# Two attentions as straight-line code, with row maxima planned closer to their use

## What is computed

```python
x = x + _layernorm(_L0_attn_ref(_layernorm(x), w_q, w_k, w_v, w_o))
x = x + _layernorm(_L0_ffn_ref(_layernorm(x), gate_w, gate_s, up_w, up_s, down_w, down_s))
x = x + _layernorm(_L1_attn_ref(_layernorm(x), Wqkv, Wo))
x = x + _layernorm(_L1_ffn_ref(_layernorm(x), W, b, A, B, p_scores))
```

## Time and profile before

| | us |
|---|---|
| median of 3 runs | 2366.73 (2365.27 to 2372.2) |
| the profiled execution, its own time | 2357.78 |
| its span, first to last instruction | 2356.0 |
| B, from the first row product (184) to 938 | 754 |
| G, from the first row product (1536) to 2145 | 609 |
| D, feed-forward of layer 0 | 460 |
| VectorE / ScalarE / TensorE busy | 1475 / 1146 / 2092 |

### The profile page before, as it was taken

The page is one execution under the profiler, slowest core; times in us unless marked ns, Lnnn a source line. Parts: engine busy times, 40 slices in busy tenths (PEclk is TensorE's granted clock), DMA queues, the critical chain, the costliest instruction groups (busy, mean ns, idle before and its releaser), DMA issues. The chain is left out here.

```text
span 2356.0 us, 39663 instructions
## 1 busy us (share of the span) xinstructions
PE 2091.7 (89%) x13072; PEld 1233.5 (52%) x13072; DVE 1475.3 (63%) x2004; ACT 1146.4 (49%) x2399; POOL 134.0 (6%) x171
## 2 busy tenths in 40 slices
PE   7987999999999998869999995789898989998785
PEld 5763333333333332748888874545455555545564
DVE  5317988887888882754333315367676666753677
ACT  3211777776777777223222211226665656663153
POOL 0000000000000000210000000000000000000203
PEclk9995999999999999979999997969998889986888
DMA  5443422422332310342100003421111111101411
GB/s 205 161 148 42 61 36 34 58 38 33 51 46 33 47 23 13 113 152 68 37 1 36 4 16 129 146 53 35 37 47 32 39 44 27 47 3 54 144 66 72
DMA packets 100890, 143.37 MB, mean 61 GB/s; under 512 B 32084, under 2 KB 43220, under 8 KB 100720
## 3 DMA queue, kind: packets, MB, share of 16 engines
q1 hardware_dynamic: 99520, 138.91, 23.2%
q10 hardware_dynamic: 832, 1.41, 0.4%
q0 software_dynamic: 384, 0.77, 0.1%
HBM read 93.45 MB, written 47.05 MB: 60 GB/s over the span
## 5 line engine op out<-in xcount | busy, mean ns | idle before, releaser
L730 DVE TENSOR_REDUCE maxesB<-s_psB 128x1 f32<-128x1024 f32 x512 | 603.1, 1220 | 116.3 <-PE s_psB L779 115.4
L714 ACT ACTIVATE probsB<-st_psB 128x512 f32<-128x512 f32 x1024 | 528.9, 603 | 171.5 <-PE st_psB L793 171.3
L730 DVE TENSOR_REDUCE maxesG<-s_psG 128x1 f32<-128x896 f32 (+7 forms) x512 | 368.9, 754 | 185.0 <-PE s_psG L764 180.5
L714 ACT ACTIVATE probsG<-st_psG 128x512 f32<-128x512 f32 (+3 forms) x768 | 335.0, 492 | 244.0 <-PE st_psG L764 180.4
L793 PE MATMUL st_psB<-q_stackB,k_stackB 50*128 50x512 f32 x1024 | 401.0, 474 | 17.2 <-ACT probsB L714 6.8
L779 PE MATMUL s_psB<-k_stackB,q_stackB 48*128 48x512 f32 x1024 | 336.7, 449 | 31.7 <-DMA k_stackB<-k_parts 18.7
L779 PE MATMUL s_psG<-k_stackG,q_stackG 52*128 52x512 f32 (+3 forms) x768 | 263.9, 426 | 65.3 <-DVE maxesG L730 38.8
L793 PE MATMUL st_psG<-q_stackG,k_stackG 54*128 54x512 f32 (+3 forms) x768 | 315.1, 463 | 6.2 <-ACT probsG L714 4.5
L779 PEld LDWEIGHTS s_psB<-k_stackB,q_stackB 48*128 48x128 f32 x1024 | 162.7, 196 | 283.8 <-DVE maxesB L730 235.9
L815 PE MATMUL o_psB<-probsB,v_onesB 128*32 128x512 f32 x2048 | 279.0, 613 | 0.0
L793 PEld LDWEIGHTS st_psB<-q_stackB,k_stackB 50*128 50x128 f32 x1024 | 169.6, 187 | 135.7 <-ACT probsB L714 132.4
(11 more groups left out here) (241 smaller groups left out, 2925.1 us busy)
## 6 DMA issues: line engine op xcount, KB each, us to landing
q_stackB<-q_parts SPq DMA_DIRECT2D x186, 64.0 KB
k_stackB<-k_parts SPq DMA_DIRECT2D x93, 128.0 KB
q_stackG<-q_parts SPq DMA_DIRECT2D x186, 64.0 KB
q_parts<-partsA SPq DMA_DIRECT2D x16, 512.0 KB, 2.8
k_parts<-partsA SPq DMA_DIRECT2D x16, 512.0 KB, 2.8
q_parts<-partsF SPq DMA_DIRECT2D x16, 512.0 KB, 2.8
k_stackG<-k_parts SPq DMA_DIRECT2D x93, 64.0 KB
xA<-in_x SPq DMA_DIRECT2D x4, 1024.0 KB
```

The costliest lines, as they stand in the source:

```text
L714: act.activation(probs[:, (i % ring) * GH + h, first:HALF], st_ps[:, bank_of(n), first:HALF], ACT.Exp).then_inc(st_used, 1)
L730: dve.reduce_max(maxes[:, half, h * QT + qt:h * QT + qt + 1], s_ps[:, n % 2, 0:key_width(half, qt)], AX.X).then_inc(maxed, 1)
```

## The change

- `run`, `body` and all loops of `attention` are gone: all 16 groups are written out, and every wait is on a constant.
- One list of steps and one of row units goes over all groups. `plan_units` gives each unit a weight (its width + 140), spreads them evenly over all steps, and starts so early that a half's maxima are ready `LEAD` = 3 steps ahead. This places 22 units ahead of the first step in B and 30 in G, then two a step in B; in G the steps of a group have 2, 6, 4, 3, 3, 2, 3, 2, 2, 1, 2, 2 units. The first unit of group `it+1` (number 32 * (it+1), for it of 1 and more) falls in step 5 of group `it` in B and in step 1 of group `it` in G. `turn_max` comes in steps 5 and 13 in B, and in G in step 1 (for half 1 of the same group) and step 5 (for half 0 of the next). For the first half of all it comes after all units that are ahead of the first step.
- `s_ps` is four slots of 512; a unit up to 512 wide takes one.
- `step_order` issues row, key and mask products by which side of the array is free; a key's masks may stand apart from it. In B the order of a step becomes R0, K2, R0', K3, K0, R1, K1, R1' (R row, K key product); before it was R0, K2, R0', K3, R1, K0, R1', K1.
- In G the row masks of TensorE go. VectorE adds a constant `ramp` (128 x 1024 float32, zero but for the mask in its last 128 columns) and takes the maximum in one operation, `tensor_tensor_reduce`, whose element output goes to `junk` in bf16. `ramp` is a new constant of 512 KB, loaded at the program's start behind `ident`.
- The copies of `o_ps` go to ScalarE in G. `v_ones` has two buffers.
- SyncE loads the stacks of group `it+1` in group `it` (before: `it+2`), once the last key product of group `it-1` is made, then V, and only then writes the rows of half 1. Group 0 loads none beside the first two.

```diff
+LEAD = 3
+FIXED = 140
+LOWEST = -3.0e38
+JUNK = 8
...
+    s_ps = ps(f"s_ps{tag}", [P, 4, HALF], F32)
+    st_ps = ps(f"st_ps{tag}", [P, n_st, HALF], F32)
...
+    def plan_units():
+
+
+        work = [key_width(t % 2, qt) + FIXED for t, qt, _ in units]
+        done = list(itertools.accumulate(work))
+        group = first_of[2]
+        per_step = done[2 * UNITS - 1] / group
+        ahead = max(done[UNITS * (t + 1) - 1] - per_step * max(first_of[t] - LEAD, 0) for t in range(1, 3))
+        ahead = max(ahead, done[UNITS - 1])
+        at = [[] for _ in steps]
+        before = []
+        for n, d in enumerate(done):
+            i = int(-(-(d - ahead) // per_step)) - 1
+            (before if i < 0 else at[min(i, len(steps) - 1)]).append(n)
+        return before, at
+
+    before, units_at = plan_units()
...
+    def step_order(i):
+
+
+        _, _, _, first, diagonal = steps[i]
+        chunks = [(n, k) for n in units_at[i] for k in range(len(row_parts(*units[n][:2])))]
+        keys = [[], []]
+        for h in range(GH):
+            keys[h // GS] += [("key", h)] + [("mask", h, a) for a in range(2) if diagonal]
+        n_rows, n_keys = max(len(chunks), 1), len(keys[0]) + len(keys[1])
+        out, free = [], [0, 0]
+        while chunks or any(keys):
+            row_side = units[chunks[0][0]][2] // GS if chunks else None
+            u = 0 if free[0] <= free[1] else 1
+            if row_side != u and not keys[u]:
+                u = 1 - u
+            rows_left, keys_left = len(chunks) / n_rows, (len(keys[0]) + len(keys[1])) / n_keys
+            if row_side == u and (rows_left >= keys_left or not keys[u]):
+                n, k = chunks.pop(0)
+                out.append(("row", n, k))
+                a, b = row_parts(*units[n][:2])[k]
+                cost = b - a
+            else:
+                out.append(keys[u].pop(0))
+                cost = HALF - first if out[-1][0] == "key" else SIDE * (out[-1][2] + 1)
+            free[u] = max(free[u], min(free)) + cost
+        return out
+
...
+    turn_after = {}
+    for t in range(TURNS):
+        i = max([j for j, ns in enumerate(units_at) if any(units[n][0] == t for n in ns)], default=-1)
+        if i >= 0:
+            turn_after[i + 1] = turn_after.get(i + 1, []) + [t]
+    early_turns = [t for t in range(TURNS) if not any(t in ts for ts in turn_after.values())]
...
-            def body(it, buf, before):
-                if before:
-                    sp.wait_ge(st_made, 1 + n_takes * it)
-                max_rows(2 * it + 1, 1, buf)
-                if not is_last(it, 2):
-                    sp.wait_ge(stacks, n_loads * (it + 2))
-                    settle(sp, sp_passed)
-                    load_stacks(sp, it + 2, (buf + 2) % 3)
-                if not is_last(it):
-                    sp.wait_ge(v_set, it + 2)
-                    settle(sp, sp_passed)
-                    load_v(it + 1)
-                if not is_last(it):
-                    max_rows(2 * it + 2, 0, (buf + 1) % 3)
-
...
+            for it in range(ITS):
+                max_rows(2 * it)
+                if it:
+                    sp.wait_ge(st_made, max(exps_of[first_of[2 * it] - 1]) + 1)
+                if it and it < ITS - 1:
+                    sp.wait_ge(stacks, n_loads * (it + 1))
+                    load_stacks(sp, it + 1)
+                if it < ITS - 1:
+                    sp.wait_ge(v_set, it + 2)
+                    load_v(it + 1)
+                max_rows(2 * it + 1)
...
+            def maximum(n):
+                t, qt, h = units[n]
+                width = key_width(t % 2, qt)
+                if n % UNITS == 0 and t >= 2:
+                    dve.wait_ge(st_made, where["max", t - 2, 0] + 1)
+                dve.wait_ge(scored, n + 1)
+                scores = s_ps[:, :, :].rearrange("p b c -> p (b c)")[:, HALF * slot_of[n]:HALF * slot_of[n] + width]
+                out = maxes[:, t % 2, h * QT + qt:h * QT + qt + 1]
+                if causal:
+                    if n >= JUNK and n % (JUNK // 2) == 0:
+                        dve.wait_ge(maxed, n - JUNK // 2)
+                    dve.tensor_tensor_reduce(junk[:, n % JUNK, 0:width], scores, ramp[:, SEQ - width:SEQ], 1.0, LOWEST, ALU.add,
+                                             ALU.max, out).then_inc(maxed, 1)
+                else:
+                    dve.reduce_max(out, scores, AX.X).then_inc(maxed, 1)
+
...
+            def row_scores(n, part):
+                t, qt, h = units[n]
+                it, half = divmod(t, 2)
+                a, b = row_parts(t, qt)[part]
+                if n % (2 * UNITS) == 0 and part == 0:
+                    pe.wait_ge(stacks, n_loads * (it + 1))
+                if part == 0 and slot_before[n] >= 0:
+                    pe.wait_ge(maxed, slot_before[n] + 1)
...
+            for n in before:
+                for part in range(len(row_parts(*units[n][:2]))):
+                    row_scores(n, part)
+            for t in early_turns:
+                turn_max(t)
+            for i, (it, half, kt, *_) in enumerate(steps):
+                if kt == 0:
+                    pe.wait_ge(m_rows, n_rows * (2 * it + half + 1))
+                for kind, *which in step_order(i):
+                    if kind == "row":
+                        row_scores(*which)
+                    elif kind == "key":
+                        key_scores(i, *which)
+                    else:
+                        mask_keys(i, *which)
+                if i:
+                    values(i - 1)
+                for t in turn_after.get(i, ()):
+                    turn_max(t)
+            values(len(steps) - 1)
```

More of the change, by code:

```diff
@@ L532, in attention @@
[L532 to L548, removed]
-        return out, [h for pair in itertools.zip_longest(*left) for h in pair if h is not None]
@@ L593, in attention @@
+    for i in range(len(steps)):
+        takes += [("exp", i, h) for h in heads_of(i)]
+        takes += [("max", t, 0) for t in turn_after.get(i, ())]
+    where = {take: n for n, take in enumerate(takes)}
+    exps_of = [[where["exp", i, h] for h in range(GH)] for i in range(len(steps))]
     n_loads = 16 * SIDES * (3 * len(Q_PARTS) + (2 if causal else 0))
     n_rows = 16 * SHIFT * SIDES
-    loop = range(1, ITS - 3)
-    assert len(loop) % 3 == 0 and n_steps % ring == 0
-    def run(engine, body):
-        body(0, 0, False)
-        with engine.Fori(0, len(loop) // 3) as i:
-            for r in range(3):
-                body(3 * i + 1 + r, (1 + r) % 3, True)
-        for it in range(ITS - 3, ITS):
-            body(it, it % 3, True)
@@ new lines, in exps @@
+            def exps(i):
+                first = steps[i][3]
+                order = heads_of(i)
+                for h in order:
+                    n = where["exp", i, h]
+                    act.wait_ge(st_made, n + 1)
+                    if h == order[0] and i >= ring:
+                        act.wait_ge(pv_done, i - ring + 1)
+                    act.activation(probs[:, (i % ring) * GH + h, first:HALF], st_ps[:, n % n_st, first:HALF],
+                                   ACT.Exp).then_inc(st_used, 1)
@@ new lines, in copy_o @@
+            def copy_o(t):
+                act.wait_ge(pv_done, first_of[t + 1])
+                act.activation(ot(*divmod(t, 2)), o_ps[:, :], ACT.Copy).then_inc(o_out, 1)
+            load_stacks(act, 0, range(1, SIDES))
+            for t in early_turns:
+                take_max(t)
+            for i, (it, half, kt, *_) in enumerate(steps):
+                exps(i)
+                if causal and kt == 0 and i:
+                    copy_o(2 * it + half - 1)
+                for t in turn_after.get(i, ()):
+                    take_max(t)
@@ L725, in _ @@
+            if causal:
+                copy_o(TURNS - 1)
         @block.vector
         def _(dve):
[L727 to L735 removed]
```

336 lines of the change are left out of this document (126 added, 210 removed).

## The result

The changed kernel takes 2523.98 us (median of 4 runs, 2521.2 to 2534.53); the kernel before took 2366.0 us beside it (4 runs, 2354.3 to 2372.2). The ratio is 1.068, with a 95% interval of 1.063 to 1.0735. Runs more than 1.5% above the fastest of the same kernel are left out of all medians and ratios here. The direction of the forecast (2480 us, +4.8%) holds; its size is 44 us short. In microseconds the value lies just inside the upper end of the range (2525); as a ratio it lies just outside (1.068, where 2525 against the 2366.73 of the forecast is 1.067).

The account below looks back on a forecast made before the run. It took coupling between engines, not one engine, as the bound. Constant +2, B -27 and G +142 gave +117 on the profiled 2357.8 us: 2475, stated as a median of 2480; range 2400 to 2525.

Parts of the forecast that it names:

- Part 1: Both attentions: written-out loops save 48 us of back-edge gaps; constants save 18 in B, G's counted in its group time.
- Part 2: Start of the attentions: fewer maxima first but an exposed first turn, B -6.7 us, G +3; larger constant +2.
- Part 3: Stack loads one group later: TensorE stands 10.5 us in each of G's groups 1 to 14, 1 us in B (+14).
- Part 4: G's group grows from 33.3 to 45.5 us through wait and lower clock, even spread saving perhaps 1.5: +171 us.
- Part 5: Fused add and maximum on VectorE: up to +6 us a group, costing nothing below the stall; keys ahead of rows: nothing.
- rival 2: Loads land in time in G and B, G's group takes 30.8 us: 2264 us; chance 0.06.
- Rival 3: The fused operation runs at half rate, G's group about 56 us: 2627 us; chance 0.04.
- Rival 1: G's stall is there, but the clock returns at once or the spread gives more, 41.4 us a group: 2421; chance 0.18.

Follow-up runs that it names:

- e3: The kernel before with only its loops written out, order, loads and masks kept: 2293.0 us, ratio 0.976.
- e5: e2 with G's causal row masks again two small TensorE products and VectorE taking only the maximum; the masks alone were priced at -15 us.
- e2: e1 with the odd half's row writes and the V load also ahead of the stacks in SyncE's queue: 2373.6 us, ratio 1.016.
- e11: e7 with the first turn of the maxima right behind the first 18 row units in B and G: 2270.1 us, ratio 0.9606.
- e1: The changed kernel with SyncE loading the stacks of group it+2, not it+1, at the start of group it: 2387.9 us, ratio 1.0145.
- e12: e2 with only the order in the step undone, in both attentions; came out near the expected 2330 us.
- e8: e2 with LEAD at 5 instead of 3: G's 14 groups took 522.6 us in the profile, against 549.6 in e2.
- e9: e6 with the row masks back on TensorE, the change's order in the step kept; undoing the order too (e7) gave 61 us.
- e6: e2 with G's row units back in the steps where the kernel before had them: 2354 us.
- e7: e2 with row-unit places, order in the step and TensorE's row masks all as in the kernel before: 2277 us.
- e10: e6 with the order in the step of the kernel before, row masks still added by VectorE: 50 us faster than e6.
- e4: The changed kernel with nine extra TensorE products ahead of its wait on the stacks in G, from group 2: 2491.2 us, ratio 1.059.
- e13: The changed kernel, loads late, with only the order in the step undone: 2526.7 us, ratio 1.066.

## Why the prediction was right in direction and wrong in size

- **Part 1 (loops written out), right in kind.** Forecast 48 + 18 + about 15 = 81; e3 measured 60 by the medians (35 to 78 by the interval of its ratio). No gap of 2 us on "issue" is left in either attention.
- **Part 2 (start), too dear by 10 us.** B's first key product came 9.0 us nearer to its first row product (forecast 6.7), G's 4.9 nearer instead of 3 further. Of these 7.9 us in G the row masks that leave its start, which I had not counted, are 1.5 (e5, with the masks back, needs 27.95 us where e2 needs 26.4), and the turn's chain is 3.0 (e11) where I had 5.5; what the rest is no run separates. That the chain is exposed there is right: e11 took 5.1 us off in B and 3.0 in G. The larger constant (+2) cost nothing: B's first row product comes at 183.1 us, before at 184.0.
- **Part 3 (late loads in G), right.** The transfers land 13.2 us behind the first issue (forecast 13.3), TensorE stands 9.65 (10.5), and from the last key to the first row product it is 13.4 us (13.4).
- **Part 3 (late loads in B), undersized.** Forecast 43.4 - 1.2 + 1.0 = 43.2 us a group; measured 44.1, 12 us over the 14. e1's groups, without the wait, take 42.3, so the wait and the clock behind it are 1.8 us, not 1.0. B's last group, which has no row products, took 44.8 against 38.8 us with the clock at 0.82: 6 more, at nothing in the forecast. e12, e8 and e9, with no wait for loads in B, had it too (0.75 to 0.78), while e6, e7 and e10 were at 1.00; it isn't the loads' doing, and what it is stays open.
- **Part 4 (G's group), the step that failed.** Its sum was 13.4 + 28.0 + 4.1 = 45.5; measured 48.65, 14 x 3.15 = 44 us. By e4, 29.2 in place of 28.0 makes 17 of these, and 6.05 in place of 4.1 for the clock 27. I had charged each group a bit over half of the 7.1 us of the earlier trace rows, and no group much more. Five of the 14 groups did better (43.3 to 44.2 us, clock 0.81 to 0.86), seven took 48.3 to 51.2 us at 0.63 to 0.71, and two 57.3 and 58.3 at 0.56 and 0.50, the last at the lower level from end to end. The stretch behind the last wait, which I had at nothing, took 41.2 against 33.0 us, with the clock at 0.67 and no wait for loads: 8 more.
- **Part 4 and Part 5 (even spread and order "nothing"), wrong, though hidden here.** I gave the spread -1.5 us a group and the order 0. With loads in time (e2) the group took 34.7 us at best where I had 30.8. The time of rival 2, 2264, was therefore wrong as well: with the loads in time the kernel takes 2374.
- **Part 5 (the fused operation), right.** 1225 ns against 1220; the accumulator read adds 83 ns, inside the bounds of nothing and +0.2. Rival 3 (half rate) is refuted (its time, by its own terms, adds up to 2630 and not 2627). The Trainium skill (Vector Engine (DVE) Microarchitecture Reference, Points that are easy to get wrong) gives half the throughput to the form of `scalar_tensor_tensor` when it has two SBUF sources that are not bf16. By its letter that spared this kernel, where one source lies in PSUM, and the trace agrees with that much. It does not agree with the rule itself: `scalar_tensor_tensor` on 512 float32 columns takes 751 ns with one tensor in PSUM (stage D) and 748 ns with both in SBUF (stage I), in the profile after:

```profile
L1123 DVE SCALAR_TENSOR_TENSOR hD<-u_psD,suD,siluD 128x512 f32<-128x512 f32 x40 | 30.0, 751 | 178.3 <-PE u_psD L73 176.0 <-ACT siluD L1083 2.3
...
L1295 DVE SCALAR_TENSOR_TENSOR yI<-mI,gammaI,yI 128x512 f32<-128x512 f32 x16 | 11.0, 748 | 0.1
```

No run has the fused add and maximum itself, or any accumulating form, with two SBUF sources.
- **Rival 1** (the clock comes back at once, 2421) did not happen, but its group time was sound: 41.4 by forecast, 42.6 in e4.

Together: 117 + 44 (G's groups) + 8 (behind the last wait) - 8 (G's start) + 17 (B: 12 + 6 + 1 in its first group - 2 at its start) - 2 (the constant) = 176 between the profiled executions; measured 177. Part 1 stands in this at its forecast, which is what the two profiled spans show (78 for 81).

That the total came within 44 us is in part luck. The forecast laid nearly the whole loss on the loads: 2480 against 2264 with them in time, 216 us. The runs give the loads 136 to 150 of it by the medians, 123 to 127 by the ratios (e1, e2). The order, the places and the masks, priced at nothing or as a gain, cost some 96 to 131 us once the loads are in time (e2 to e7), and show nothing for the order (e13) while they are late.

Step by step, by the medians and in brackets by the ratios: before to e3 -60 (-57), loops; to e7 -16 (-35), start, loads, copies; to e2 +96 (+131), order, places, masks; to e1 +14 (-4), rows behind the loads, not clear of noise; to the change +136 (+127), loads late.

What stays open is what exactly makes the clock fall in e2 and its relatives, where TensorE never stands for 2 us behind G's first key product. It is not the longest gap alone: e12, with eight waits of 2.0 to 3.2 us in G, has the higher clock (0.84 against 0.77). The small mask products that left TensorE bear on it (e10 0.87, e7 0.94 with them back), but the runs do not show why one group falls and the next, the same, does not.

## What to carry to other kernels

Before a prefetch is moved, compare the time from its release to its landing with the time from the release to its first reader, stage by stage: here the same edit made TensorE wait 1.2 us a group in B, where the first reader stands in step 5, and 9.5 in G, where it stands in step 1. The order in which products enter TensorE's queue can be a cost of its own (here 37 to 71 us): let each product that may wait for a bank stand beside one that need not, and measure it with the larger wait removed, because under a larger wait it shows nothing. And moving small work off TensorE is no gain by itself: here it took 0.5 us off a group at full clock and yet cost 26 us in the whole kernel (e7 to e10), so price it together with the granted clock of the stretch.

## What the runs showed of the hardware that was not expected

Code without a single wait over 2 us ran at a mean clock of 0.77 through 15 groups of G (e2, the first line), while e12, with the same work in another order and eight such waits, ran at 0.84 (the second), and e3, with the old places and TensorE's masks besides, at 1.00 in 14 of its groups:

```profile
1527.70:2116.40 588.70, 534.05 (x3895) 259.48 (x3894) 351.14 (x952) 338.58 (x810) 17.82 (x45) 0.77 0.14 33
```

```profile
1533.10:2079.60 546.50, 487.71 (x3897) 247.69 (x3895) 343.52 (x954) 338.40 (x811) 17.79 (x45) 0.84 0.16 36
```

In e6 nine groups in a row had the lower level for about their first half and the upper for the second:

```profile
1871.80:1889.40 17.60, 17.39 (x105) 8.07 (x105) 10.01 (x29) 9.65 (x24) 0.74 (x2) 0.55 0.33 73
1889.40:1909.30 19.90, 17.38 (x161) 8.98 (x160) 13.28 (x36) 13.04 (x31) 0.44 (x1) 0.97 0.02 5
```

In its first half TensorE was busy for 17.39 of 17.60 us at the low level; being busy did not bring the clock back at once. And products added only to fill a wait (e4) did not make the kernel slower: by the medians it was 33 us faster (22 by the ratios, not clear of noise), with G's groups at 0.89 in place of 0.72.
